# Moving the segment borders of an edge stage: 22, 22, 18, 10, 10, 7, 7 and 5 groups instead of 21, 21, 18, 10, 10, 7, 7 and 7

## What is computed

```
h   = x @ W_in + b_in
Wij = (ssp(edge_attr @ Wf1 + bf1) @ Wf2 + bf2) * edge_weight     # one row of 128 per edge
agg = segment_sum(h[idx_j] * Wij, idx_i)                         # idx_i = src, idx_j = dst
x   = layernorm(x + ssp(agg @ Wo1 + bo1) @ Wo2 + bo2)
# then a graph attention layer over the same edges (softmax over each destination's edges), and a second layernorm
```

## Time and profile before

| | us |
|---|---|
| median of 3 runs | 1375.3 |
| lowest and highest run | 1372.75, 1376.11 |
| the profiled execution | 1371.59 |
| its span, first to last instruction | 1369.6 |
| mean granted PE clock (share of full speed) | 0.93 |

### The profile page before, as it was taken

One profiled execution on the slowest core, in us unless ns is written; L12 is line 12 of the kernel. 1 busy time (PEld: TensorE's weight loads), 2 busy tenths in 40 slices (PEclk: granted clock), 3 DMA queues, 4 the chain that ended last, 5 costly groups with the idle time before them and its releaser, 6 DMA issues. The chain is left out here.

```text
span 1369.6 us, 27977 instructions
## 1 busy us (share of the span) xinstructions
PE 1155.7 (84%) x8980; PEld 938.9 (69%) x9072; DVE 1182.4 (86%) x2186; ACT 917.4 (67%) x2210; POOL 873.8 (64%) x945
## 2 busy tenths in 40 slices
PE   5786787798899977899978999999999595888995
PEld 4543455457778756788766877777777494888995
DVE  7798976649899978899978999999998668999976
ACT  2564675568788987698977888788877134544523
POOL 3377777777777777777777777777777501334511
PEclk9697998899999999999999999999999898879998
DMA  8232342266899478899698988999898785678761
GB/s 258 76 98 82 87 132 80 78 161 173 236 258 255 155 232 220 233 252 244 193 270 225 280 237 231 245 286 239 246 260 222 198 227 174 202 232 268 267 212 38
DMA packets 246565, 276.09 MB, mean 202 GB/s; under 512 B 35079, under 2 KB 194470, under 8 KB 243078
## 3 DMA queue, kind: packets, MB, share of 16 engines
q1 hardware_dynamic: 197762, 183.84, 45.7%
q0 software_dynamic: 25792, 53.29, 12.3%
q10 hardware_dynamic: 22852, 37.02, 12.3%
HBM read 162.85 MB, written 111.20 MB: 200 GB/s over the span
## 5 line engine op out<-in xcount | busy, mean ns | idle before, releaser
L1977 POOL DMA_INDIRECT edge_rows<-x_rows,pos x806 | 778.8, 966 | 250.5 <-issue 229.5
L1475 ACT ACTIVATE h_edge<-ps_wh,w_col 128x128 f32<-128x128 f32 x808 | 229.3, 367 | 105.9 <-PE ps_wh L1276 98.8
L1320 PEld LDWEIGHTS ps_d<-back_one,back 128*128 128x128 f32 x1914 | 232.1, 193 | 61.4 <-issue 57.8
L1320 PE MATMUL ps_d<-back_one,back 128*128 128x128 f32 x1914 | 241.2, 278 | 4.7 <-DVE agg_t L1794 4.2
L1283 PE MATMUL ps_wh<-wf,filt 128*128 128x128 f32 x1616 | 233.5, 289 | 0.6 <-DVE filt L1577 0.5
L1269 PE MATMUL ps_v<-f_t,wf 128*128 128x512 f32 x400 | 223.1, 641 | 0.0
L1581 DVE TENSOR_TENSOR x_rows<-ps_wh,h_edge 128x512 f32<-128x512 f32 x202 | 137.9, 683 | 86.2 <-DMA edge_rows<-x_rows,pos 45.3
L1283 PEld LDWEIGHTS ps_wh<-wf,filt 128*128 128x128 f32 x1616 | 204.1, 198 | 2.6 <-DVE filt L1577 2.6
L1112 PE MATMUL ps_wh<-yard 128*128 128x150 bf16 x1575 | 138.0, 233 | 61.6 <-DVE yard L1102 39.8
L1112 PEld LDWEIGHTS ps_wh<-yard 128*128 128x128 bf16 x1575 | 108.7, 100 | 107.1 <-DVE yard L1102 84.3
L2470 PE MATMUL ps_wh<-loan,yard 128*126 128x129 f32 x1250 | 154.5, 288 | 26.0 <-DVE yard L2756 15.3
(11 more groups left out here) (354 smaller groups left out, 1423.6 us busy)
## 6 DMA issues: line engine op xcount, KB each, us to landing
c_tab<-yard SPq DMA_DIRECT2D x25, 1575.0 KB
yard<-c_tab SPq DMA_DIRECT2D x25, 1575.0 KB, 6.7
dst_bc<-dst ACTq DMA_DIRECT2D x99, 252.0 KB
back<-edge_rows SPq DMA_DIRECT2D x42, 516.0 KB, 9.3
edge_rows<-x_rows,pos POOLq DMA_INDIRECT x806
back<-edge_rows SPq DMA_DIRECT2D x48, 258.0 KB, 5.1
m_tab<-yard SPq DMA_DIRECT2D x25, 393.8 KB
mask_room<-m_tab SPq DMA_DIRECT2D x5, 1968.8 KB, 12.9
```

The lines of the kernel that those rows point to most:

```text
L1320: mm = nc.tensor.matmul(acc(c), back_rows(n)[:, k0 + t, 0:D], back_one[:, m % 2, o + t, :], start=t == 0, stop=t == k1 - k0 - 1, skip_grou ...
L1475: copy = nc.scalar.activation(h_edge[:, j, q, :], ps_wh[:, bank, 1, q * D:(q + 1) * D], ACT.Copy, scale=w_col[:, t(q)])
L1977: return pool.indirect_dma_start(table[s], bass.IndirectOffsetOnAxis(places_here, 0), rows, None)
```

## The change

The borders and the tiles of the last segment change, and nothing else:

```
-GS = (0, 21, 42, 60, 70, 80, 87, 94, NG)
+GS = (0, 22, 44, 62, 72, 82, 89, 96, NG)
 NS = len(GS) - 1
-KS = (8, 8, 7, 4, 4, 3, 3, 3)
+KS = (8, 8, 7, 4, 4, 3, 3, 2)
```

## The result

The kernel before takes 1375.22 us (median of 17 runs), the changed one 1379.03 us (17 runs): ratio 1.0031, 95% interval 1.0024 to 1.0038, 3.8 us slower. The forecast of 1375.4 was 3.6 us too low; the time lies inside the range, inside what the prediction called no change (4.1 us), and clear of noise it is slower.

The account below looks back on a forecast made before the run. POOL's scatter issue was taken to bound the kernel until 1085.5, then the chain to PE's late sums. Later by 6.4 + 0.2, back 6.5: +0.1 us, forecast 1375.4 us; own range 1372.5 to 1379.5, 8-in-10 range 1370.5 to 1381.

Parts of the forecast that it names:

- Up to the last product: Scatter stream before half 201: POOL's 806 issues keep its end at 1085.5; five sets fewer gain 0.4 us at most, taken as 0.
- T: Start of the last product, in half 201: 1072.34 before the change, at least 1069.4 after it, taken as 1070.8.
- The tail: Sets behind the last product: four more, no longer hidden, start the first late one-hots near T + 28.8, 6.4 us later.
- SP's queue: Last segment's window loads: ten go out behind the last gather, then residual rows and late loads; nothing late, 0.2 us added.
- SP is too late: Slower rival: ten loads behind the last gather land too late for the sets, up to +5 us, 1380; chance 0.23.
- The late sums: Five sums after the late loads: ten passes fewer each; with the first one-hot block 6.5 us back, first two 7.2 us shared.
- The rule against the change: PE's exit from the stage: instruction fetch after a taken branch meets the late loads; 0.35 us worse, left in the range.

Follow-up runs that it names:

- the first of the last two kernels: Changed kernel with mid-kernel exit at half 91, SP's late addresses read right after, ACT's late loads without the memset, residual add after second one-hots: 1372.47 us (0.9985).

## Why the prediction was right, and where it was wrong

The forecast was within its range, and most of its tail held. That the time fell inside is in part luck: the range got its width from late landings and other terms of the tail, and the 3.8 us came from a term held at 0.4 at most. Of the prediction's signs, the last scatter came at 1092.4 instead of 1084 to 1086, the fifth sum ended 8.7 us later instead of within 2 us, and two signs of being wrong were seen, POOL waiting for products and DVE waiting for read-back rows. The step that failed is the one ahead of the tail: "Five sets fewer before half 201 can only raise a lead that all but suffices: 0.4 us at most, taken as 0", and with it "POOL's 806 issues stay, so 1085.5 stays". The issues stayed, the lead did not.

*Up to the last product.* The prediction looked for the closest pair near the end and found it at half 189; there the lead did rise (0.78 to 2.07 us), and without the exit in the way the scatter stream from half 40 on is indeed 0.4 to 2.0 us shorter than with the old boundaries. It listed that sets move from halves 92-121 to 96-125 and did not set this beside the exit in mid-kernel, whose cost it had in the earlier trace rows and used only as a price for the tail. Two losses of lead of 5 to 6 us each, the start of the read-backs and the exit, had been nine halves apart and were now five. The gaps show 2.66 us of it (2.3 and 4.9 in two other traces with these boundaries and this exit), and moving the exit either way returns the time. The medians give 4.4 us, 2.8 to 6.0; the 2.66 of this trace lies just below, but its whole stream from half 40 on is 4.1 us longer than with the exit at half 91. The rest beyond the gaps is spread over many halves, and no cause is shown for it.

*T.* Taken as 1070.8; 1078.07 less the 7.9 us of the later stream is 1070.2.

*The tail.* In the changed kernel with the earlier exit, where the stream doesn't disturb it, the terms are these: the last add at T + 20.3 (forecast 20.1), the memset at T + 23.55 (23.4), the residual add ending at T + 28.5 (28.8), and the first late one-hots at T + 28.9 (28.8). Its rows:

```profile
1098.04 0.06 DVE L1970 MEMSET conv_end<- 1x1 f32 x1 [3.27 <-issue]
1099.46 3.49 DVE L2696 TENSOR_TENSOR yard<-yard,ps_d 126x3200 f32<-126x3200 f32 x1 [1.36 <-PE ps_d L2423]
1103.35 0.18 DVE L2649 SCALAR_TENSOR_TENSOR late_lo<-last_away,yard 128x10 f32<-128x10 f32 x1 [0.40 <-DMA yard<-edge_rows]
```

Both limits that the prediction named, the residual add and ACT's late loads, end within 0.4 us of each other, and from POOL's last issue to the end of the fifth late add the tail came out 0.5 us longer than before (41.1 against 40.6). Forecast was +0.1 in all. In the changed kernel itself the limits lie 1.7 us apart, and the tail is 1.1 us longer than before (41.7).

*SP's queue.* Ten loads behind the last gather sufficed but for 0.77 and 0.99 us in the changed kernel, and without any wait in the trace with the earlier exit (0.20 and 0.91 with the later one). The rival "SP is too late" happened in small. What the prediction missed is the residual rows: it gave them ten us until their use and did not ask what their 1575 KB meet on the way. They meet the last scatters, which then land up to 6.7 us behind the start of their issue instead of 2.6. SP's fifteen late loads, said to "start when the last scatter landed", start 5.8 us behind the end of the last issue instead of 1.9, also because their addresses are read behind the residual rows. In the changed kernel that is hidden behind the set tail and the residual add.

*The late sums.* 6.5 us back forecast; the sums show 6.9 less than before (14.0 against 20.9) and the kernel with three tiles 7.8 more. The first two took 6.19 us (7.2 forecast; 7.37 with the earlier exit).

*The rule against the change.* The exits show something like it in their size. DVE stood 3.55 to 8.14 us at the same exit in mid-kernel, in thirteen traces. It was 7.75 to 8.14 in the three where SP's store of a count table (1575 KB) went out 2 to 3 us ahead, 5.63 in the changed kernel, and 3.55 to 4.44 in the nine others; the DMA share while DVE stood was 0.62 to 0.77, 0.30, and 0.16 to 0.27. The five kernels in which SP reads its late addresses right behind the exit test this without having been meant to: they hold that store back until DVE is through, or 0.3 us before, at the same half 91. The store and DVE's exit with the earlier exit alone, then in the first of the last two kernels:

```profile
512.43 0.38 SPq L1155 DMA_DIRECT2D c_tab<-yard  x1
523.54 0.41 DVE L1572 TENSOR_SCALAR onehot_t<-dst_bc,base_p,win_off 126x512 bf16<-126x512 int16 x1 [8.14 <-issue]
```

```profile
519.57 0.38 SPq L1156 DMA_DIRECT2D c_tab<-yard  x1
517.63 0.41 DVE L1574 TENSOR_SCALAR onehot_t<-dst_bc,base_p,win_off 126x512 bf16<-126x512 int16 x1 [3.55 <-issue]
```

At the end of the stage it was 5.82 us with all late loads in flight. The Trainium skill ("Runtime: NRT & Kernel Launch", Instruction fetch mechanics) lets a taken branch whose target isn't loaded wait for a DMA that fetches it, and the traces fit it: the instruction queues move 0.05 to 0.09 MB around the mid-kernel exits. But 3.41 us stands beside late loads in flight too, and the register reads are part of the exit in mid-kernel, so what the time at an exit is made of is not settled. Taken as 0.35 us in the tail and nothing in mid-kernel, the exit was weighed in the wrong place.

## What to carry to other kernels

When a change moves work in time, lay its new place beside every fixed event (exits from a block, segment starts, large loads and stores), not only beside the bottleneck's closest pair: two stalls that a buffer absorbs one at a time can together drain it. A lead is a stock, and the distance that lets it grow back is part of the schedule. And when a step has two limits that end close together, price both, since removing one gives back only the distance to the other; and ask of each moved transfer whose landing it delays.

## What the runs showed of the hardware

- One exit from a block kept DVE idle from 3.55 to 8.14 us, longest where a store of 1575 KB was in flight (DMA share 0.62 to 0.77), and cost nothing of the kernel's time where the lead was larger.
- A load of 1575 KB issued among indirect scatters moved their last landing from 2.3 to 2.6 us to 6.7 us behind the start of their issue; the same load behind 25 others took 13.7 and 15.6 us.
- SP took about 0.6 us for each address that it read from SBUF: 9.55 us lie between the residual rows and the first late load, with fifteen reads between.
